# Layer-norm chain, first codes and integer parts around the quantized feed-forward product

## The reference

```python
x = x + xattn(layernorm(x), ctx, ctx, WQ, WK, WV, WO, mask)   # 32 batches, 100 tokens, D = 256, 16 heads, 361 keys
x = x + ffn(layernorm(x), W1, b1, W2, b2)                     # hidden width 1024

def affine_quantize(x):                  # one scale over the whole tensor
    scale = max((max(x) - min(x)) / 255, 1e-8)
    zp = clip(round(-min(x) / scale) - 128, -128, 127)
    q = clip(round(x / scale) + zp, -128, 127)
def qlinear(x, W, b):
    return einsum((xq - zx), wq) * (sx * sw) + b
def ffn(x): return qlinear(gelu(qlinear(x, W1, b1)), W2, b2)
```

## Time and profile before

| | us |
|---|---|
| median of 3 runs | 1071.03 |
| lowest and highest run | 1069.54, 1071.66 |
| profiled execution | 1068.56 |
| its span, first to last instruction | 1066.7 |
| PE busy | 1022.7 (96%) |
| DVE busy | 935.2 (88%) |
| ACT busy | 860.5 (81%) |
| POOL busy | 768.2 (72%) |

### The profile page before, as it was taken

One profiled execution on the slowest core, in us unless ns is written; L12 is line 12 of the kernel. 1 busy time (PEld: TensorE's weight loads), 2 busy tenths in 40 slices (PEclk: granted clock), 3 DMA queues, 4 the chain that ended last, 5 costly groups with the idle time before them and its releaser, 6 DMA issues.

```text
span 1066.7 us, 38212 instructions
## 1 busy us (share of the span) xinstructions
PE 1022.7 (96%) x10935; PEld 657.5 (62%) x10935; DVE 935.2 (88%) x2673; ACT 860.5 (81%) x1810; POOL 768.2 (72%) x1098
## 2 busy tenths in 40 slices
PE   8999999999999999999999999999999999997728
PEld 6664666666666666666666666666666666664317
DVE  7877888888888889888888888888888888886997
ACT  5756888888888888888888888888888888876906
POOL 3356778777887777788877778877877878774700
PEclk9999999999999999999999999999999999999969
DMA  8503876666676677766667777667766666763003
GB/s 246 140 1 54 144 138 136 137 138 137 137 141 137 139 142 142 139 137 138 137 137 142 142 142 141 137 137 140 142 137 137 140 140 135 140 126 129 1 0 124
DMA packets 435439, 136.80 MB, mean 128 GB/s; under 512 B 407666, under 2 KB 434390, under 8 KB 435414
## 3 DMA queue, kind: packets, MB, share of 16 engines
q1 hardware_dynamic: 435414, 136.47, 61.7%
HBM read 28.60 MB, written 6.55 MB: 33 GB/s over the span
## 4 chain that ended last, share of the span: by engine, by line
PE 89%; DVE 7%; issue 1%; DMA 1%; ACT 1%; POOL 0%; ACTq 0%; DVEq 0%; SPq 0%; POOLq 0%
PE front L370 21%; PE front L372 18%; PE front L371 18%; PE back L1370 13%; PE front L1348 7%; PE tp L1348 5%; DVE hrange L1161 3%; DVE hrange L1162 3%; PE back L370 1%; PE back L372 1%; PE back L371 1%; DMA xs<-x 1%; PE front L1485 1%; PE tp L1485 1%; PE back L1485 0%
## 5 line engine op out<-in xcount | busy, mean ns | idle before, releaser
L620 POOL TENSOR_TENSOR hl<-prob,hl 100x361 f16<-100x361 f32 x511 | 429.4, 856 | 73.1 <-ACT hl L759 72.4
L753 ACT ACTIVATE prob<-prob,nmax 100x361 f32<-100x361 f32 x512 | 295.4, 590 | 4.9 <-DVE nmax L1008 3.7
L1370 PEld LDWEIGHTS back<-v,pT 128*128 128x128 f16 (+1 forms) x4608 | 167.8, 98 | 32.3 <-issue 9.5
L759 ACT ACTIVATE hl<-prob 100x361 f16<-100x361 f32 x352 | 175.3, 498 | 3.4
L1370 PE MATMUL back<-v,pT 128*128 128x65 f16 (+1 forms) x4608 | 176.9, 193 | 0.8 <-DMA pT<-hl 0.8
L763 ACT ACTIVATE k_h<-front 128x362 f16<-128x362 f32 x256 | 120.3, 470 | 63.6 <-PE front L372 59.7
L370 PE MATMUL front<-ctx_h,wk_h 128*128 128x362 f16 x512 | 164.0, 320 | 1.6 <-DVE v L1068 1.0
L372 PE MATMUL front<-ctx_h,wk_l 128*128 128x362 f16 x512 | 161.7, 316 | 0.0
L371 PE MATMUL front<-ctx_l,wk_h 128*128 128x362 f16 x512 | 161.4, 315 | 0.0
L1068 DVE SCALAR_TENSOR_TENSOR v<-front,v 128x512 f16<-128x512 f32 (+1 forms) x192 | 132.8, 692 | 32.3 <-ACT v L767 31.5
L767 ACT ACTIVATE v<-front 128x512 f16<-128x512 f32 (+1 forms) x192 | 114.6, 597 | 55.4 <-PE front L372 49.7
(11 more groups left out here) (217 smaller groups left out, 2060.5 us busy)
## 6 DMA issues: line engine op xcount, KB each, us to landing
ctx_raw<-ctxT SPq DMA_DIRECT2D x33, 361.0 KB, 3.2
pT<-hl SPq DMA_TRANSPOSE x253, 3.6
xs<-x SPq DMA_DIRECT2D x8, 400.0 KB
q_all<-x SPq DMA_DIRECT2D x32, 100.0 KB
out<-q_all SPq DMA_DIRECT2D x32, 100.0 KB
xb<-out SPq DMA_DIRECT2D x5, 640.0 KB, 8.5
out<-xb SPq DMA_DIRECT2D x25, 128.0 KB, 1.8
q_all<-wq SPq DMA_DIRECT2D x1, 1024.0 KB, 6.7
```

The source lines that it names most:

```text
L620: pool.tensor_tensor(hl[0:T, n % RT, 1, 0:S], prob[0:T, n % RP, 0:S], hl[0:T, n % RT, 0, 0:S], ALU.subtract).then_inc(s_lo, 1)
L753: act.activation(prob[0:T, n % RP, 0:S], prob[0:T, n % RP, 0:S], ACT.Exp, bias=nmax[0:T, n:n + 1], scale=-1.0).then_inc(s_exp, 1)
L759: act.activation(hl[0:T, h % RT, 0, 0:S], prob[0:T, h % RP, 0:S], ACT.Copy).then_inc(s_ha, 1)
L1370: ins = pe.matmul(obank[j % 2][:, n % GH * DV:(n % GH + 1) * DV], pT[0:r, n % RT, part_ * ST + st, :], v2[half][0:r, st, v, n % HT, :], st ...
```

## The change

- Last layer norm: EPS is added on VectorE (RS 0), GpSimd keeps the power (POW), VectorE applies mean and reciprocal root to the two extremes (YX), folds them (LM), and only then makes the shift (RS 1), for which ScalarE's YN waits. YM is gone from ScalarE, LE stands before the last WO steps. The other 31 batches keep their steps.
- Block 0 of y: VectorE makes the integers of its first half, between 1/scale and the clamp limits, ScalarE those of the second half, ahead of its three blocks. VectorE clamps the halves separately, and TensorE transposes the first half before the second.
- The first GELU (g = 0) is split in two of 400 columns; its halves wait for their own two matmuls.
- Declarations of new semaphores (s_rv, s_rp, s_yf, s_hp) are left out of the diff.
- Integers of the GELU output: columns 0 to 127 by VectorE (again between 1/scale and the limits), 128 to 399 by ScalarE in two parts, c = 1 by GpSimd in two halves, c = 2, 4, 6 by ScalarE and c = 3, 5, 7 by GpSimd. All clamps stay on VectorE.

```diff
@@ -46,17 +46,19 @@
 NQ = 4
 NT = B * T // P
 NX = 5
-CD = 3
+HPARTS = [(0, P, "DVE"), (P, 2 * P, "ACT"), (2 * P, TW, "ACT"), (TW, TW + TW // 2, "POOL"), (TW + TW // 2, 2 * TW, "POOL")] + [
+    (c * TW, (c + 1) * TW, "ACT" if c % 2 == 0 else "POOL") for c in range(2, NB)]
+HBY = {by: [(first, last) for first, last, e in HPARTS if e == by] for by in ("DVE", "ACT", "POOL")}
 CUT = 10
 PADS = 5
 HT = H // 2
...
@@ -154,14 +156,14 @@
     ("AT", 2), ("AT", 3), ("WO", 1)]
 LAST_ACT = [
     ("HA", 7), ("EXP", 12), ("AH", 0), ("EXP", 13), ("HA", 8), ("EXP", 14), ("HA", 9), ("EXP", 15),
-    ("HA", 10), ("PC", 11), ("PC", 13), ("AH", 1), ("AC", 0), ("AH", 2), ("AC", 1), ("AH", 3), ("YM", 0), ("YN", 0)]
+    ("HA", 10), ("PC", 11), ("PC", 13), ("AH", 1), ("AC", 0), ("AH", 2), ("AC", 1), ("AH", 3), ("YN", 0)]
 LAST_DVE = [
     ("MAX", 14), ("MAX", 15), ("HV", 4), ("PC", 10), ("DL", 14), ("PC", 12), ("PC", 14), ("PC", 15),
-    ("NORM", 2), ("NORM", 3), ("DAL", 3), ("AC", 2), ("AC", 3), ("WO", 0), ("WO", 1), ("LN", 0), ("LN", 1),
-    ("LX", 0), ("LX", 1), ("LE", 0), ("LM", 0), ("LM", 1)]
+    ("NORM", 2), ("NORM", 3), ("DAL", 3), ("AC", 2), ("AC", 3), ("LE", 0), ("WO", 0), ("WO", 1), ("LN", 0),
+    ("LN", 1), ("RS", 0), ("LX", 0), ("LX", 1), ("YX", 0), ("LM", 0), ("LM", 1), ("RS", 1)]
 LAST_SP = [("X", 0), ("OUT", 0)]
 LAST_POOL = [
-    ("LO", 10), ("M", 0), ("LO", 11), ("LO", 12), ("LO", 13), ("LO", 15), ("AL", 0), ("AL", 1), ("AL", 2), ("RSTD", 0)]
+    ("LO", 10), ("M", 0), ("LO", 11), ("LO", 12), ("LO", 13), ("LO", 15), ("AL", 0), ("AL", 1), ("AL", 2), ("POW", 0)]
 def order(events, part, last):
...
@@ -623,6 +625,9 @@
                     wait_alone(pool, s_ah, NG * a + n + 1)
                     pool.tensor_tensor(ahl[0:T, n, 1, :], att[0:T, n % 2, :], ahl[0:T, n, 0, :],
                                        ALU.subtract).then_inc(s_al, 1)
+                elif kind == "POW":
+                    pool.wait_ge(s_rv, 1)
+                    pool.tensor_tensor(row[0:T, 9:10], row[0:T, 8:9], mhalf[0:T, 0:1], ALU.pow).then_inc(s_rp, 1)
                 elif kind == "RSTD":
                     wait_alone(pool, s_ln, LN_STEPS * a + 2)
                     pool.tensor_scalar(row[0:T, 8:9], row[0:T, 7:8], EPS, None, ALU.add).then_inc(s_rl, 1)
...
@@ -675,6 +680,12 @@
         for c in range(NX):
             x1 = xb2[:, c * NT // NX:(c + 1) * NT // NX, :]
             pool.tensor_tensor(x1, x1, b2r[:, :].unsqueeze(1).broadcast_to([P, NT // NX, D]), ALU.add).then_inc(s_xb, 1)
+        pool.wait_ge(s_dve, 12)
+        for first, last in HBY["POOL"]:
+            pool.tensor_scalar(hq[:, :, first:last].bitcast(I16), hid[:, first // TW, :, first % TW:first % TW + last - first],
+                               sc[:, INV2:INV2 + 1], 1.0, ALU.mult, ALU.mult).then_inc(s_hp, 1)
     @block.scalar
...
@@ -782,13 +793,11 @@
                     wait(act, s_wp, 2 * a)
                     act.activation(attT[:, n, :, 0:T], att_bank[n][:, 0:4 * T].rearrange("p (c t) -> p c t", c=4),
                                    ACT.Copy).then_inc(s_aca, 1)
-                elif kind == "YM":
-                    wait(act, s_rl, 3 * a + 3)
-                    wait(act, s_ln, LN_STEPS * a + 4)
-                    act.activation(row[0:T, 12:14], row[0:T, 10:12], ACT.Identity, scale=row[0:T, 9:10],
-                                   bias=row[0:T, 8:9]).then_inc(s_ym, 1)
                 elif kind == "YN":
-                    wait(act, s_rl, 3 * a + 3)
+                    if part != "last":
+                        wait(act, s_rl, 3 * a + 3)
+                    else:
+                        act.wait_ge(s_rv, 2)
                     act.activation(yn_slot(a), x1_slot(a), ACT.Identity, scale=row[0:T, 9:10],
                                    bias=row[0:T, 8:9]).then_inc(s_yn, 1)
                 elif kind == "MG":
...
@@ -821,6 +830,8 @@
         act.activation(rinv[0:T, 0:1], rinv[0:T, 0:1], ACT.Gelu)
         act.wait_ge(s_dve, 4)
+        act.activation(y16_block(0)[:, TB // 2:TB, :].bitcast(I16), yn_block(0)[:, TB // 2:TB, :], ACT.Identity,
+                       scale=sc[0:T, INV1:INV1 + 1]).then_inc(s_ya, 1)
         for c in (1, 2, 3):
             act.activation(y16_block(c).bitcast(I16), yn_block(c), ACT.Identity,
                            scale=sc[0:T, INV1:INV1 + 1]).then_inc(s_ya, 1)
...
@@ -833,16 +844,17 @@
         for pair in range(NP2):
             for m in range(NF):
                 g = pair * NF + m
-                act.wait_ge(s_f1, g + 1)
-                act.activation(hid[:, 2 * pair:2 * pair + 2, m, :], wide[g % 3][:, :, 0:TW], ACT.Gelu,
-                               bias=b1c[:, m:m + 1], scale=sc[:, S1:S1 + 1]).then_inc(s_ge, 1)
+                for n in ((0, 1), (1, 2)) if g == 0 else ((0, 2),):
+                    act.wait_ge(s_f1, g + 1 + int(n[1] == 2))
+                    ins = act.activation(hid[:, 2 * pair + n[0]:2 * pair + n[1], m, :], wide[g % 3][:, n[0]:n[1], 0:TW],
+                                         ACT.Gelu, bias=b1c[:, m:m + 1], scale=sc[:, S1:S1 + 1])
+                ins.then_inc(s_ge, 1)
                 if m in (4, 5) and pair < NP2 - 1:
                     y_out(2 * pair + m - 2)
         act.wait_ge(s_dve, 12)
-        for c in [c for c in range(NB) if c != CD]:
-            ts = slice(0, TW // 2 if c == 0 else TW)
-            act.activation(hq[:, :, c * TW + ts.start:c * TW + ts.stop].bitcast(I16), hid[:, c, :, ts], ACT.Identity,
-                           scale=sc[:, INV2:INV2 + 1]).then_inc(s_h1, 1)
+        for first, last in HBY["ACT"]:
+            act.activation(hq[:, :, first:last].bitcast(I16), hid[:, first // TW, :, first % TW:first % TW + last - first],
+                           ACT.Identity, scale=sc[:, INV2:INV2 + 1]).then_inc(s_h1, 1)
     @block.vector
...
@@ -1035,7 +1047,20 @@
                 elif kind == "LX":
                     wait(dve, s_x1, 2 * a + 2)
                     dve.tensor_reduce(row[0:T, 10 + n:11 + n], x1_slot(a), AX.X, (ALU.max, ALU.min)[n]).then_inc(s_ln, 1)
+                elif kind == "RS":
+                    if n == 0:
+                        wait(dve, s_ln, LN_STEPS * a + 2)
+                        dve.tensor_scalar(row[0:T, 8:9], row[0:T, 7:8], EPS, None, ALU.add).then_inc(s_rv, 1)
+                    else:
+                        dve.tensor_scalar(row[0:T, 8:9], row[0:T, 6:7], row[0:T, 9:10], -1.0, ALU.mult,
+                                          ALU.mult).then_inc(s_rv, 1)
+                elif kind == "YX":
+                    wait(dve, s_ln, LN_STEPS * a + 4)
+                    dve.wait_ge(s_rp, 1)
+                    dve.tensor_scalar(row[0:T, 12:14], row[0:T, 10:12], row[0:T, 6:7], row[0:T, 9:10], ALU.subtract,
+                                      ALU.mult).then_inc(s_ym, 1)
                 elif kind == "LE":
+                    wait(dve, s_ln, LN_STEPS * a)
                     dve.tensor_reduce(red[0:T, 0, :], ext[0:T, 0:B - 1, :].rearrange("p b w -> p w b"), AX.X,
                                       ALU.max).then_inc(s_le, 1)
                 elif kind == "LM":
...
@@ -1118,31 +1143,40 @@
         wait(dve, s_ln, LN_STEPS * B + 2)
         dve.sem_inc(s_rd, 1)
-        def quant_scalars(g, inv, lo, hi):
+        def quant_scalars(g, inv, lo, hi, meanwhile):
             dve.wait_ge(s_ar, g + 1)
             link(dve.tensor_reduce(glob[:, g, :], tp[0][:, 0:2 * P].rearrange("p (w n) -> p w n", w=2), AX.X, ALU.max))
             link(dve.tensor_tensor(col(SPAN), glob[:, g, 0:1], glob[:, g, 1:2], ALU.add))
             link(dve.tensor_scalar(col(SPAN), col(SPAN), 1.0 / 255.0, 1e-8, ALU.mult, ALU.max))
             link(dve.reciprocal(col(inv), col(SPAN)))
+            meanwhile()
             link(dve.tensor_scalar(col(ZP), glob[:, g, 1:2], col(inv), MAGIC, ALU.mult, ALU.add))
             link(dve.tensor_scalar(col(ZP), col(ZP), -MAGIC, 0.0, ALU.add, ALU.max))
             link(dve.tensor_scalar(col(lo), col(ZP), 255.0, -1.0, ALU.min, ALU.mult))
             link(dve.tensor_scalar(col(hi), col(lo), 255.0, None, ALU.add))
-        quant_scalars(0, INV1, LO1, HI1)
+        def y_ints():
+            dve.tensor_scalar(y16_block(0)[:, 0:TB // 2, :].bitcast(I16), yn_block(0)[:, 0:TB // 2, :],
+                              sc[0:T, INV1:INV1 + 1], None, ALU.mult).then_inc(s_yd, 1)
+        quant_scalars(0, INV1, LO1, HI1, y_ints)
+        def clamp_y(y):
+            return dve.tensor_scalar(y, y.bitcast(I16), sc[0:T, LO1:LO1 + 1], sc[0:T, HI1:HI1 + 1], ALU.max, ALU.min)
         def y_codes(c):
             y = y16_block(c)
             if c == 0:
-                dve.tensor_scalar(y.bitcast(I16), yn_block(c), sc[0:T, INV1:INV1 + 1], None, ALU.mult).then_inc(s_yd, 1)
                 dve.wait_ge(s_yd, 1)
+                clamp_y(y[:, 0:TB // 2, :]).then_inc(s_yf, 1)
+                dve.wait_ge(s_ya, 1)
+                clamp_y(y[:, TB // 2:TB, :]).then_inc(s_yq, 1)
             else:
-                dve.wait_ge(s_ya, c)
```

(52 more changed lines are left out.)

6 lines of the change are left out of this document (3 added, 3 removed).

## The result

| | before | after |
|---|---|---|
| median of seven runs, us | 1071.03 | 1079.0 |
| lowest and highest run | 1069.54, 1072.0 | 1075.88, 1080.57 |
| span of the profiled execution | 1066.7 | 1077.2 |

A forecast was written before the change was run, and what follows sets the result against it. VectorE was taken to bound the kernel until 1037 us, then TensorE: +3.15 us from GELU integers on three engines, -0.4 from layer norm and halves, so 1071.03 + 2.75 = 1073.8 us, range 1068.9 to 1075.6.

The forecast's parts named there:

- What bounds the kernel: Last stages: VectorE bounds 981.5 to 1037 us, then TensorE; early gains only advance the first reduce, the third place counts fully.
- Layer norm and halves: Chain before the first reduce: layer norm gain of 0.85 us shrinks to 0.1 at ScalarE; with halves 0.4, bounds 0.1 and 0.8.
- The third part: GELU integers on three engines: VectorE and GpSimd exclude each other per instruction; last block 3.15 us later; case chance 0.42.
- my two conflicts (c = 5 and c = 7): Second product: GpSimd's c = 5 and c = 7 hold up VectorE, stalling TensorE 2.8 us before block 9, 1.0 before block 12.
- The walk: Step-by-step timing of the last stage under the exclusive port: last block starts at 1066.15 against 1063.0, +3.15 us.
- The sum: Whole kernel: profiled 1068.56 us + 3.15 - 0.4 = 1071.3; as median 1071.03 + 2.75 = 1073.8 us.
- No keeping out: Rival, last stage: VectorE's clamps and GpSimd's integers run side by side; gain 1.65 us in all, 1069.4 us; chance 0.32.
- GpSimd keeps the port through all five: Rival, last stage: clamp 0 and TensorE start only at 1051.4; +9.3 - 0.4 us, 1079.9 us; chance 0.08.
- VectorE wins the port between two GpSimd instructions: Rival, last stage: c = 3 clamped at 1048.4, stalls of 0.2, 0.9 and 0.9 us; +1.0 us, 1072.0 us; chance 0.12.
- What would show it: Trace signs: GpSimd's first int16 instruction 2 us, clamps 2 to 3 us, TensorE idle over 2 us before blocks 9 and 12.

The follow-up runs named there:

- e7: Kernel before with only the last layer norm's new order; moments to first reduce 10.59 us against 11.70; 1067.55 us in one run, against 1068.42 beside it.
- e6_warm: Changed kernel plus 6, 20, 20 and 20 dummy matmuls before blocks 1 to 4 of the second product; last stage 88.43 us against 91.24; 1075.26 us, one run.
- e2_third_only: Kernel before with only the GELU integers split over three engines; 1078.55 us, ratio 1.0071; last stage 90.54 us.
- e12_no_pool_warm: Changed kernel with zeros for GpSimd's integers and 11 dummy matmuls instead of 3 behind the third scale operation; last stage 80.24 us; 1066.62 us, one run.

## Why the prediction failed, step by step

**What bounds the kernel: right.** The gain of the first two places did arrive only as an earlier first reduce, and the third place counted in full.

**Layer norm and halves: right in kind, too small.** Predicted 0.4 us, with bounds of 0.1 and 0.8; measured 1.13, outside them. The missing 0.73 sits in the wait for ScalarE. I let YN start 0.26 later than before, behind the new shift; it started 2.64 us after the moments, 0.11 earlier than before (974.35 - 971.71 against 972.59 - 969.84), in the main because the 0.33 us gap between the folds that I kept was gone. That is 0.37. Small ones bring it to 0.78: ScalarE's integers start 0.09 before the dummy GELU's end and its GELUs 0.09 before the integers' end, the integers take 3.82 for my 3.93 and the three GELUs 2.14 for my 2.26; 0.05 is lost again between the steps. The mechanism had a fault too. I let ScalarE's lateness behind the table load shrink the layer norm's gain of 0.85 to 0.1, with the halves to make up for it. e7 has the old division of block 0 and the full 1.11 us: its first GELU waits for VectorE's copy and TensorE, not for ScalarE (0.74 us of idle time). It is the halves, with half a block more on ScalarE, that put ScalarE last in the changed kernel, and they bring 0.02.

**The third part: the mechanism was right, the turn-taking wrong.** "Whoever runs first keeps the other out to the end of its instruction" held in each row. What failed is the next step: "Clamps 1 and 2 follow to 1042.0. In the gap behind them GpSimd takes part 4, to 1043.4." I assumed that VectorE keeps the port as long as its clamps follow without a gap, and that GpSimd gets in only between them. In the trace GpSimd's next instruction starts 0.29 to 0.45 us before the running clamp ends (1041.59 against 1041.89), VectorE's next only 0.08 before it (1041.81), and GpSimd goes first. (That the earlier start decides is not shown: at 979.00 it didn't, see the last section.) So each of the first five clamps paid for one GpSimd instruction: TensorE waited before blocks 1 to 4, for 0.61, 2.06, 2.17 and 1.33 us, and not before 9 and 12. By the time of my two conflicts (c = 5 and c = 7) GpSimd was through, at 1052.74. The walk gave +3.15 us; the waits measured 6.97.

The Trainium skill's page "SBUF — State Buffer", section "Who interferes with whom", calls the pair of ports an exclusive lock that the first to issue holds for the whole instruction. The rows agree (1.81 us for a clamp of 1024 elements). My rule for who comes next when both have work queued was my own, read into one row (979.00 in the earlier trace rows), and it was worth 3.8 us here.

**The clock: a term that was missing.** I had no cost for TensorE's clock behind the waits. It was 2.81 us (e6_warm), and 2.1 in e2_third_only by its blocks 4 to 7 (5.61 us for 3.49). Even with the waits walked rightly, the sum without it would have been short.

**The sum.** 6.97 + 2.81 - 1.13 = 8.65 us over before; the medians differ by 7.97, in agreement within what runs of one kernel differ (1075.88 to 1080.57). My 2.75 was the sum of three terms, all of them too small in size: -0.4 for -1.13, +3.15 for +6.97, 0 for +2.81.

**The rivals.** "No keeping out" had 0.32 and fell: no clamp of the first five ran at its own length. Its price was right all the same: it gave the third part a gain of 1.25 us, and e12_no_pool_warm, in which GpSimd is out of the stage, gained 1.22 (80.24 for 81.46), with 8 more dummy matmuls to hold the clock. "GpSimd keeps the port through all five" gave 1079.9, within a microsecond of the median, for a reason that the trace refutes: clamp 0 came at 1041.89, not at 1051.4, and the two engines alternated. That the time came out close is luck in part: its 9.3 us were one long wait before block 0, where the trace has no loss before block 0, 6.97 us of waits behind it and 2.81 of the clock. "VectorE wins the port between two GpSimd instructions" is nearest in kind, alternation, and I gave it 1072.0 because I let it begin only at c = 3.

**What would show it.** Right: GpSimd's first int16 instruction at 2.15 us for 1.6, clamps of 1600 elements at 3.06 and 3.30, the integers of y behind the dummy GELU. Wrong: the place of the stalls.

## What to carry to other kernels

When work is given to GpSimd beside a VectorE that clamps and converts back to back, as here, count one whole GpSimd instruction ahead of every such VectorE instruction for as long as GpSimd's queue holds work, not only where the two happen to collide. (A row at 979.00 in the earlier trace rows shows one clamp that didn't pay.) If the work must go there, cut it into short instructions (800 elements in place of 3200 took the loss from 9.8 to 0.5 us here, the clock's share included). When waits of 2 us appear in front of TensorE, price the clock behind them as well, or fill them. And of two edits to one chain, try each alone: here one of them carried the whole gain, and the other, worth 0.55 us alone, added nothing to it.
